# Masked attention on one core: half of the weights turned by 32x32 blocks on VectorE and through memory, values copied and contexts cast by ScalarE

## What is computed

```python
Q = query @ Wq.T + bq;  K = key @ Wk.T + bk;  V = value @ Wv.T + bv     # 16 heads of 16
energy = einsum('bhqd,bhkd->bhqk', Q, K) / sqrt(16)
energy = where(mask == 0, -1e20, energy)
attention = softmax(energy, axis=-1)
x = einsum('bhqk,bhkd->bhqd', attention, V)
return x.transpose(0, 2, 1, 3).reshape(b, -1, 256) @ Wo.T + bo
```

## Time and profile before

| | us |
|---|---|
| median of 3 runs (lowest, highest) | 1988.75 (1988.57, 1992.19) |
| the profiled execution | 1987.96 |
| its span, first to last instruction | 1986.2 |
| TensorE busy | 1941.3, 98% |
| VectorE busy | 1232.3, 62% |
| ScalarE busy | 1112.4, 56% |
| GpSimd busy | 600.2, 30% |
| loop over batches, energies(0) to energies(31) | 975.42 to 1233.59 |
| in it: VectorE, ScalarE busy | 220.45, 200.47 |

### The profile page before, as it was taken

The page is one execution under the profiler, slowest core; times in us unless marked ns, Lnnn a source line. Parts: engine busy times, 40 slices in busy tenths (PEclk is TensorE's granted clock), DMA queues, the critical chain, the costliest instruction groups (busy, mean ns, idle before and its releaser), DMA issues.

```text
span 1986.2 us, 43991 instructions
## 1 busy us (share of the span) xinstructions
PE 1941.3 (98%) x17307; PEld 1694.8 (85%) x17307; DVE 1232.3 (62%) x3579; ACT 1112.4 (56%) x2432; POOL 600.2 (30%) x652
## 2 busy tenths in 40 slices
PE   6999999999999998998999999999999999999998
PEld 6898998989898984777688887889999999999998
DVE  7767777776767666776688988438758623243212
ACT  5666666666666663333577877544444444444443
POOL 3111141112211101233122211444444444444444
PEclk9999999999999999999999999999999999999999
DMA  5656454455445431000311011001010010101000
GB/s 202 185 174 205 148 166 151 151 174 151 158 152 166 144 123 48 1 1 1 92 43 37 25 33 40 6 1 64 1 43 22 22 43 1 43 1 43 1 12 32
DMA packets 100332, 154.21 MB, mean 78 GB/s; under 512 B 12896, under 2 KB 78752, under 8 KB 100000
## 3 DMA queue, kind: packets, MB, share of 16 engines
q1 hardware_dynamic: 100128, 151.41, 24.3%
HBM read 103.73 MB, written 43.45 MB: 74 GB/s over the span
## 4 chain that ended last, share of the span: by engine, by line
PE 46%; ACT 2%; DVE 2%; issue 1%; POOL 0%; POOLq 0%; DVEq 0%; ACTq 0%
PE bank L83 21%; PE bank L1132 18%; PE bank L1053 2%; PE bank L1068 1%; PE bank L1040 1%; ACT att_p L1238 1%; PE bank L1098 1%; PE bank L1009 1%; ACT att_pt L1243 1%; PE bank L1079 0%; DVE dec_room L140 0%; POOL right_h L963 0%; ACT att_kt L1230 0%; PE bank L1091 0%; DVE att_vz L1385 0%
## 5 line engine op out<-in xcount | busy, mean ns | idle before, releaser
L963 POOL TENSOR_TENSOR right_h<-right_hr,right_h 128x512 fp32r<-128x512 f32 x256 | 340.9, 1332 | 418.3 <-ACT right_hr L1285 418.3
L1284 ACT ACTIVATE right_h<-bank,dec_b 128x512 fp32r<-128x512 f32 x256 | 176.3, 689 | 389.6 <-PE bank L83 365.0
L83 PE MATMUL bank<-lat_kv_t,lat_qk 128*128 128x320 f32 x1536 | 253.7, 314 | 2.8 <-DVE lat_qk L2456 2.8
L83 PE MATMUL bank<-lat_wv,lat_kv_t 128*128 128x512 f32 x960 | 242.1, 393 | 0.0
L83 PEld LDWEIGHTS bank<-lat_kv_t,lat_qk 128*128 128x128 f32 x1536 | 227.6, 188 | 15.5 <-DVE lat_qk L2456 6.4
L2320 ACT ACTIVATE lat_p<-bank,lat_neg_max 128x320 f32<-128x320 f32 x256 | 134.6, 527 | 148.4 <-DVE lat_neg_max L2461 148.4
L83 PEld LDWEIGHTS bank<-lat_wv,lat_kv_t 128*128 128x128 f32 x960 | 175.1, 188 | 30.4 <-DVE lat_qk L2456 0.4
L83 PE MATMUL bank<-dec_xt,dec_lo 128*128 128x512 f32 x512 | 200.7, 392 | 0.0
L2461 DVE TENSOR_REDUCE lat_neg_max<-bank 128x1 f32<-128x320 f32 x256 | 122.5, 486 | 93.6 <-PE bank L83 87.6
L1285 ACT ACTIVATE right_hr<-bank,dec_b 128x512 f32<-128x512 f32 x256 | 174.4, 681 | 0.0
L1132 PE MATMUL bank<-dec_hi,right_h 128*128 128x256 f32 x1024 | 161.6, 280 | 1.2 <-POOL right_h L963 1.2
(11 more groups left out here) (332 smaller groups left out, 3806.6 us busy)
## 6 DMA issues: line engine op xcount, KB each, us to landing
lat_turns<-lat_pb SPq DMA_DIRECT2D x63, 640.0 KB, 3.0
lat_pt<-lat_turns SPq DMA_DIRECT2D x252, 160.0 KB, 3.2
raw_w<-in_L_ffn_W SPq DMA_DIRECT2D x16, 1024.0 KB, 6.6
lat_ctx_raw<-in_ctx SPq DMA_DIRECT2D x16, 512.0 KB, 5.3
right_ctx_raw<-in_ctx_turned SPq DMA_DIRECT2D x16, 512.0 KB, 3.7
lat_kv_f<-in_ctx_turned SPq DMA_DIRECT2D x15, 512.0 KB, 4.3
lat_ctx_raw<-gate_rows SPq DMA_DIRECT2D x15, 512.0 KB, 4.8
lat_kv_t<-lat_lt SPq DMA_DIRECT2D x32, 128.0 KB, 4.4
```

Of the source, the lines that this page charges most:

```text
L83: mm = pe.matmul(out, lhs(a, k), rhs(b, k), start=first and k == 0 and n == 0, stop=last and k == KD - 1 and n == 2)
L963: pool.tensor_tensor(h[:, g % 2, 1, :], hr[:, g % 2, :], h[:, g % 2, 0, :].bitcast(F32), ALU.subtract).then_inc(h_lo, 1)
L1284: act.activation(h[:, n % 2, 0, :], h_bank[n % 2][:, :], ACT.Relu, bias=bias).then_inc(h_hi, 1)
```

## The change

The first half of the weights (m = 0) of batches 0 to 30 is no longer turned by TensorE. VectorE turns its 32x32 blocks in two pieces (`turn(b, half)`), a transfer a piece takes them to a tensor in memory, `att_turns`, and four transfers a piece bring them back with the blocks in place, in `pt_early`. `pt_early` has one buffer: the fetch waits for the products of the batch before. The exponentials of half 0 are written over their scores. `weigh(b)` is one step at the slot's end, one slot after `energies(b)` as before. The second half of the weights and all of batch 31 stay with TensorE.

The values' bias is left out of the values and goes into the output bias once: `bv` is loaded as columns, spread over `ot` and multiplied by Wo in slot 0, and VectorE adds the result to `bo`. So the values are only copied, which ScalarE does, to a `vz` of three buffers instead of two; from batch 1 on they are computed in `pt_bank[0]` instead of `proj_bank`. ScalarE also casts the contexts. On VectorE `normalise(b-1)` stands last in the slot; on TensorE `project_output` is in odd slots and ahead of the projections.

```diff
@@ SyncE
+            def weights_out(b, half):
+                sp.wait_ge(p_turned, 2 * b + half + 1)
+                if half == 0:
+                    wait(sp, pt_in[b % 2], 128 * (b // 2))
+                sp.dma_start(turns[b % 2, half], pb[:, half].rearrange("p g u c -> p (g u c)")).then_inc(p_out[half], 16)
+
+            def weights_back(b, half):
+                sp.wait_ge(p_out[half], 16 * (b + 1))
+                if half == 0:
+                    wait(sp, o_psum, b)
+                for g in range(4):
+                    sp.dma_start(pt_early[g * 32:(g + 1) * 32, half].rearrange("p q r t c -> p q (r t c)"),
+                                 turns[b % 2, half].rearrange("(q p) (g c) -> g p q c", q=4, g=4)[g]).then_inc(pt_in[b % 2], 16)
...
-            for i in range(2, NT):
-                context(i)
+            context(2)
+            for b in range(B - 1):
+                for half in range(2):
+                    weights_out(b, half)
+                for half in range(2):
+                    weights_back(b, half)
+                if b % 2 == 1 and (b + 5) // 2 < NT:
+                    context((b + 5) // 2)
@@ TensorE
             def turn(b, m):
+                u = turn_of(b, m)
                 for half in range(2):
                     pe.wait_ge(p_ready, 8 * b + 4 * m + 2 * half + 2)
-                    if 2 * b + m >= 1:
-                        pe.wait_ge(pt_done, 2 * (2 * b + m) - 1 + half)
-                    if m == 1 and half == 1 and b in in_slot:
+                    wait(pe, pt_done, 2 * u - 1 + half)
+                    if half == 0:
+                        pe.wait_ge(v_done, min(b + 2, B))
+                    if half == 1 and u < B and b in in_slot:
                         pe.wait_ge(*read_out(*in_slot[b]))
...
+            def weigh(b):
+                pe.wait_ge(pt_done, 2 * turn_of(b, 1) + 2)
+                if b < B - 1:
+                    pe.wait_ge(pt_in[b % 2], 128 * (b // 2 + 1))
+                pe.wait_ge(v_done, b + 1)
...
             for b in range(B):
                 energies(b)
+                if b == 0:
+                    output_bias()
                 if b >= 1:
                     turn(b - 1, 1)
+                if b >= 3 and b % 2 == 1:
+                    project_output((b - 3) // 2)
                 if b + 1 < B:
                     keys_proj(b + 1)
-                if b >= 1:
-                    weigh(b - 1, 0)
-                    weigh(b - 1, 1)
-                turn(b, 0)
-                if b + 1 < B:
                     values_proj(b + 1)
                 if b in in_slot:
-                    pe.wait_ge(pt_done, 4 * b + 2)
+                    pe.wait_ge(pt_done, 2 * b)
                     side_step(*in_slot[b])
-                if b >= 2 and b % 2 == 0:
-                    project_output(b // 2 - 1)
+                if b >= 1:
+                    weigh(b - 1)
             pe.wait_ge(s_low, 8 * B)
             hidden(0, 0)
+            turn(B - 1, 0)
             turn(B - 1, 1)
@@ ScalarE
+            def split_keys(i):
+                if i >= 2:
+                    act.wait_ge(ctx_in[i % 2], 16 * (i // 2))
+                    act.wait_ge(v_psum, 2 * i - 2)
+                act.copy(ctx_t[:, i % 2, 0], ctx_raw[:, i % 2]).then_inc(c_hi, 1)
+
+            def values_proj(b):
+                act.wait_ge(v_psum, b + 1)
+                wait(act, o_psum, b - 2)
...
+                for par in range(2):
+                    at = par * W32
+                    ins = act.copy(to[:, :, at:at + HD], src[:, :, par, :])
+                ins.then_inc(v_done, 1)
...
             rows_turned(1)
+            act.wait_ge(consts, 1)
+            values_proj(0)
             act.wait_ge(pre, 1)
             queries(0)
...
-                weights_of(b, 0, 0)
-                if b >= 1:
-                    turn(b - 1, 1)
-                for r in range(1, R):
-                    weights_of(b, 0, r)
+                for half in range(2):
+                    for r in (2 * half, 2 * half + 1):
+                        weights_of(b, 0, r)
+                    if b >= 1:
+                        turn(b - 1, 1, (half,))
                 if b + 1 < B:
                     keys_proj(b + 1)
-                turn(b, 0)
+                if b % 2 == 0 and b // 2 + 1 < NT:
+                    split_keys(b // 2 + 1)
                 for r in range(R):
+                    if b + 1 < B and r == 2:
+                        values_proj(b + 1)
                     weights_of(b, 1, r)
@@ VectorE
+            def turn(b, half):
+                dve.wait_ge(p_ready, 8 * b + 2 * half + 2)
+                wait(dve, p_out[half], 16 * b)
+                dve.transpose(pb[:, half], p[0][:, 2 * half:2 * half + 2].rearrange("p r (t g c) -> p g (r t) c", g=4, c=32)
+                              ).then_inc(p_turned, 1)
...
                 slot_head(b)
+                lowest(b, 0, 0, R)
                 if b >= 3 and b % 2 == 1:
                     residual(b // 2 - 1)
-                lowest(b, 0, 0, R)
-                lowest(b, 1, 0, R)
-                if b % 2 == 0 and b // 2 + 1 < NT:
-                    split_keys(b // 2 + 1)
+                if b < B - 1:
+                    turn(b, 0)
+                lowest(b, 1, 0, 2)
+                if b < B - 1:
+                    turn(b, 1)
+                lowest(b, 1, 2, R)
+                if b == 0:
+                    output_bias()
                 if b % 2 == 1:
                     add_bias(b // 2)
+                slot_early(b)
+                slot_late(b)
                 if b >= 1:
                     normalise(b - 1)
-                slot_early(b)
-                if b + 1 < B:
-                    values_proj(b + 1)
-                slot_late(b)
```

More of the change, by code:

```diff
@@ L890, in _ @@
                 sp.dma_start(mask_i[half * S:(half + 1) * S, :], w["mask_1x1xSxS2_ik1"]).then_inc(loads, 16)
-            for t in range(2):
-                sp.dma_start(bv[:, t, :], everywhere(w["L1_xattn_bv"])).then_inc(loads, 16)
+            with nc.allow_non_contiguous_dma(reason="a bias as a column"):
+                sp.dma_start(bv[:, :], column(w["L1_xattn_bv"])).then_inc(loads, 16)
             sp.dma_start(bo[:, :], everywhere(w["L1_xattn_bo"])).then_inc(loads, 16)
@@ L1053, in turn, with output_bias @@
                             mm = pe.transpose(pt_bank[half][:, (2 * n + t) * P:(2 * n + t + 1) * P],
-                                              p[:, m, 2 * half + n, t * P:(t + 1) * P], k.ident[:, :])
+                                              p[m][:, 2 * half + n, t * P:(t + 1) * P], k.ident[:, :])
                     mm.then_inc(pt_psum, 1)
[L1057 to L1060, removed]
-                    if b >= 1:
-                        pe.wait_ge(o_read, b)
-                if m == 0 and b >= 2:
-                    pe.wait_ge(x_att, b // 2)
[L1065 to L1072, removed]
+            def output_bias():
+                pe.wait_ge(bv_cols, 1)
+                for m in range(KD):
+                    mm = pe.matmul(projected(0), ot[:, 0, m, :], wo[:, m, :], start=m == 0, stop=m == KD - 1)
+                mm.then_inc(bv_psum, 1)
@@ new lines, in weigh @@
+            def weigh(b):
[4 more added lines that the diff above has]
+                if b == 0:
+                    pe.wait_ge(bo_whole, 1)
+                if b >= 1:
+                    pe.wait_ge(o_read, b)
+                if b >= 2:
+                    pe.wait_ge(x_att, b // 2)
+                for m in range(KD):
+                    for par in range(2):
+                        for t in range(2):
+                            for r in range(R):
+                                to = weighted[r * W32:(r + 1) * W32, m, :, par, :]
+                                of = vz[:, b % 3, t, m, r, par * W32:(par + 1) * W32]
+                                if m == 0:
+                                    mm = pe.matmul(to, of, pt_early[:, r // 2, 2 * par:2 * par + 2, r % 2, t, :], start=t == 0, stop=t == 1)
+                                else:
+                                    mm = pe.matmul(to, of, pt_late[:, r, t, par * S:(par + 1) * S], start=t == 0, stop=t == 1)
+                mm.then_inc(o_psum, 1)
```

99 lines of the change are left out of this document (57 added, 42 removed).

## The result

The change makes the kernel slower: 2000.0 us in the median of 4 runs (1998.9 to 2002.8) against 1989.0 of the kernel before in the same session, a ratio of 1.0058 with a 95% interval of 1.0046 to 1.0069. The forecast was 1982.8, its range ended at 1997.

The account below looks back on a forecast made before the run. TensorE, busy 98% of the span, was taken as the bound. Gains of 1.5 (light) and 7 (heavy) less 2.5 paid made 6.0 us off 1987.96, so 1982.0; the median 0.8 above, 1982.8; range 1973 to 1997.

Parts of the forecast that it names:

- the light stretch: Batches 1 to 10, attention alone, 75.03 us before: five slot pairs gain between +3 and -0.5 us, 1.5 taken.
- opening and end: Around the batch loop: 1.1 us lost at the start, 0.5 for the last turn, 0.95 for the projection; 2.5 paid.
- the price of the context load: SyncE's queue: the load makes every second transfer out land after 4.2 us instead of 3.0; odd weigh slips 0.7.
- the way through memory: Weights out and back: from one weigh's end 5.7 us to the last landing, so no slot under 6.75 us.
- the heavy walk: Batches 11 to 30, with side work: batches 11 to 22 walked, 99.8 against 105.2 us; 0.45 a slot, 7 taken.
- Removing the turn: TensorE, batches 0 to 30: the early half's turn goes, 31 x 0.85 = 26.4 us.
- VectorE: Two 128x512 transposes a batch added at 0.71 us each; net +0.32 to +0.35 a batch, heavy stretch 162.8 us of work.
- rival D: The change doesn't do what it says, e.g. VectorE's transposes run at half rate: 2005 us or more; chance 0.03.
- ScalarE: Cast 0.95 us, value copies 0.75; its 6.6 us chain in even slots makes TensorE wait 0.45 for the remaining turn.
- rival B: Slower by the round trip: landings summing above 6.9 us, light slot pairs 16.0 us, kernel 1998; chance 0.17.
- floor of 168 us by VectorE: Heavy stretch: VectorE's 162.8 us of work plus waits allow nothing under 168, so at most 9.4 us gain.
- Rival C: No change: handovers between three nearly full engines eat the heavy slots' gain; 1988, between 1985 and 1993; chance 0.30.

Follow-up runs that it names:

- ctx_small: Changed kernel with the loads of contexts 3 to 15 cut to 8 of their 512 columns; 1987.5 us, 0.9998 of the kernel before.
- cast_dve: Changed kernel with the context cast back on VectorE, behind the last `lowest` of the slot; 2011.3 us, 1.0112 of the kernel before.
- ctx_after_out: Changed kernel with whole context loads moved between the transfers out and the fetches of even batches; 1989.3 us, 1.0002 of the kernel before.
- mid_open: Changed kernel with one transfer out, four back; output projection between keys' and values' products; residual behind last `lowest`; ScalarE's first values behind its first queries; 1986.6 us.
- short_turns: `mid_open` with VectorE's transposes of batches 2 to 30 cut from 128x512 to 128x32, waits and transfers kept; 1974.8 us, 0.9923.
- whole: Changed kernel with one 512 KB transfer out and four 128 KB fetches a batch instead of two and eight; 1988.1 us, 0.9994.

## Why the prediction was wrong

Term by term, in the profiled executions: the light stretch was to gain 1.5 us and lost 6.1, the heavy one was to gain 7 and lost 0.8, opening and end were to cost 2.5 and cost 3.2, and 2.4 more lie ahead of the changed code. So two steps failed, with nearly 8 us each: the price of the context load on the way through memory, and the heavy walk.

Removing the turn: right in the light stretch. With the clock at 1.00 (`ctx_small`) TensorE's busy time there falls by 9.5 us, and ten turns and one projection are 9.45. In the changed kernel itself the fall over both stretches is 26.2 us (6.6 and 19.7); that it equals the 26.4 of the forecast is luck, since the slower instructions of four slots count as busy, and the heavy stretch falls by 20 where twenty turns are 17; for that excess no run shows a cause.

VectorE: right in size. The transpose takes 708 ns, 0.71 was drawn from its two neighbours. The heavy stretch has 161.2 us of VectorE against the 162.8 of the sum. The rival D falls with it.

ScalarE: the cast takes 1.05 us, not 0.95, and the value copies 0.65 a pair, not 0.75; they cancel. That its chain would hold the turn in odd slots was wrong as the limit: TensorE has no wait of its own for an exponential ahead of the turn (its weight loads have 3.3 us of it), against 23.1 us ahead of `weigh`, and `cast_dve` gained nothing in the light stretch.

The way through memory: here the prediction failed. It priced the fetches from the end of weigh, 5.7 us, and let the context load cost every second transfer out a landing of 4.2 instead of 3.0, a slip of 0.7 in the odd slots. The landings of the fetches were better than assumed, 2.0 us, and so were those of the transfers out with no load ahead, 2.0 to 2.6 us in the light stretch. But behind a load they were 4.4 to 5.9, not 4.2, so the load adds some 2.5 us and not 1.2. Left out as well was SyncE's order: the transfer out of an even batch cannot be issued before the eight fetches of the batch before and the load are, 1.6 us after its data are ready in slot 4. And eight issues took 5.1 us there instead of 3.5; that isn't the load's doing, as `ctx_small` has 5.3 in the same slot without it, and its cause is open. In slot 5 the way from the end of one weigh to the next took 9.1 us, not 5.7 nor 6.4: 2.3 until the transfer out had landed, 5.1 of issue, 1.7 to the last landing. So the odd light slots average 9.4 us (slots 3, 5, 7, 9) where 7.5 to 8.2 was said, and the even ones 7.3 instead of 6.75. `ctx_after_out` takes the load out of the way, and 10.8 of the 11 us are back. The passage of the Trainium skill that the prediction weighed there, "DMA: Bandwidth & Descriptors", section "Anatomy of one DMA", gives its 2 us for transfers that GpSimd issues. Here SyncE issued them, and 64 KB landed after 2.0 us and 256 KB after 2.1 (`ctx_small`); what the sum lacked is not in it.

That is close to rival B, which had the context load in the queue, light pairs of 16.0 us and 1998; the four pairs of slots 2 to 9 average 16.8. Its condition, landings that sum to 6.9 us or more, was met or nearly so behind the loads (4.4 to 5.9 and 2.0) and not elsewhere (4.0 to 4.6), and it had not the late issue. The chance of 0.17 for it was too low: the prediction itself said that the load stands between the fetches and the next transfer out, and never walked SyncE's queue as it walked the engines'.

The clock: left out altogether. The granted clock is 1.00 in all of this stage before the change; after it TensorE, idle for 3 us in slot 5 with waits in the slots before, is granted 0.87, 0.75, 0.86 and 0.84 in slots 5, 6, 25 and 27. These are mixtures of the two levels, 2.4 and 1.2 GHz: twice what lacks to 1.00, times the slot, makes 13.6 us at the lower one. Slot 6 shows the price where TensorE is the bound: 7.9 us for 6.1 us of work. The Trainium skill, "TensorE: Matmul & The Clock Gate", section "HAM oscillation — how this bites in real kernels", says that waits for data between short pieces of work let the clock fall again and again; the trace agrees in kind, with falls in 4 of the loop's 31 slots. A step that turns TensorE's work into TensorE's waits should have had this among its rivals. How much of the 11 us it cost is not shown; `ctx_small` and `ctx_after_out` have the clock at 1.00 in every slot of the light stretch, so what they give back includes the clock's share there.

The heavy stretch: no kernel with the full transposes came under the floor of 168 us by VectorE, but the hand walk was wrong. It had 0.45 us a slot gained; the changed kernel has 0.04 lost, and with the round trip and the clock repaired (`mid_open`) 0.13 gained, 174.8 against 177.4. The walk covered slots 11 to 22 and was stretched to twenty. For those it said 99.8 us; `mid_open` takes 102.5, and gains 2.7 on the kernel before there. Slots 23 to 30, which were not walked, take 72.3 us where they took 72.2: they gained nothing, and the walk's mean gave them 3.6. VectorE's lateness isn't absorbed as assumed: `short_turns` gives back 11.2 us for 24.5 us of work taken away. This is the step that would have been wrong even without the queue. With VectorE busy for 93% of the stretch in `mid_open` and three engines that hand work to one another in each slot, the stretch stays 7 us above the floor of its busiest engine. Rival C, no change, describes the repaired kernel.

Opening and end: right. 1.6 us lost in the opening (1.1 was said), 1.6 behind the loop (1.45 was said). A further 2.4 us of the profiled execution lie ahead of the changed code, about as much as profiled executions of one and the same code there differ by (2.3 us); the ratio of the medians doesn't rest on that execution alone.

## What to carry to other kernels

A queue that issues transfers is an engine in order like the others: walk it with each issue's length, and ask what stands ahead of the transfer that someone waits for. A prefetch that nobody is in a hurry for belongs behind the urgent transfer, whose landing it delays more than its issue does. Fewer, larger transfers keep the queue short. Work taken off the busiest engine was worth almost nothing here, where the engine that took it over came to 90% of its stretch, and in four slots the freed engine idled and then ran at a lower clock. When a walk covers a part of the stretch, its mean holds for that part.

## What the runs showed of the hardware

The landing of a transfer depends little on its size up to half a megabyte when nothing stands ahead: 64 KB fetched 2.0 us, 128 KB fetched 2.9 (in `whole`), 256 KB out 2.1 (in `ctx_small`), 512 KB out 2.7 to 3.0 (in `whole`, for the light stretch's odd batches). It depends a good deal on what was issued just before it: the same 256 KB behind a 512 KB load took 4.4 to 5.9. Eight issues of 64 KB fetches took 3.65 us in some slots and up to 5.1 in others (5.3 in `ctx_small`), so the time of an issue isn't fixed either; single ones took up to 2.1 us. And a clock that has fallen shows in the lengths of the instructions: 16 instructions of `energies` 1.15 and 2.09 us, 8 of `turn` 1.09 and 1.97.
